# Rotating the query without normalising it, in a local attention of a three-part network

## What is computed

```python
def l2norm(t):
    return t / jnp.clip(jnp.linalg.norm(t, axis=-1, keepdims=True), 1e-12)

qkv = shift_token(x) @ wqkv                     # 8 heads of 64
q, k, v = to_heads(split(qkv))
q = l2norm(q) * qs
k = l2norm(k) * ksc
q, k = rotary_xpos(q, k)        # t * cos * scale + rotate_half(t) * sin * scale
# windows of 64, each looks at itself and the window before it
sim = einsum('bhwid,bhwjd->bhwij', q * 8, k)    # masked by a band
attn = softmax(sim)
out = einsum('bhwij,bhwjd->bhwid', attn, v)
```

## Time and profile before

| | |
|---|---|
| median of 3 runs | 1942.15 us (1931.54 to 1948.5) |
| profiled execution, its own time | 1935.09 us |
| its span | 1933.0 us |
| TensorE, VectorE, ScalarE, GpSimd busy | 81%, 65%, 51%, 58% |
| mean granted TensorE clock | 0.915 of full speed |

### The profile page before, as it was taken

How to read it: one execution, slowest core, us unless ns; L and a number is a source line. 1 busy time by engine, 2 the same in 40 slices (tenths; PEclk the granted TensorE clock), 3 DMA queues, 4 the chain that set the end, 5 groups by cost and what they waited for, 6 DMA issues and landing times.

```text
span 1933.0 us, 31789 instructions
## 1 busy us (share of the span) xinstructions
PE 1569.3 (81%) x12145; PEld 1057.8 (55%) x12153; DVE 1251.9 (65%) x2158; ACT 977.6 (51%) x2359; POOL 1116.3 (58%) x1069
## 2 busy tenths in 40 slices
PE   5688787878788968787989787889797689899866
PEld 3354454546555645465656454656564367677535
DVE  6665564678777855797768557877685454354345
ACT  3266557525555654255465642554656354444333
POOL 0000000777777747777777467777774777777700
PEclk8999899989999989899989988999998799899866
DMA  4010001434333344333334343334343633333311
GB/s 162 5 24 17 14 21 39 111 100 118 115 109 110 116 90 104 97 114 118 107 99 119 77 116 101 105 116 120 101 118 76 181 109 98 103 100 102 102 17 44
DMA packets 93420, 178.72 MB, mean 92 GB/s; under 512 B 21452, under 2 KB 50264, under 8 KB 93016
## 3 DMA queue, kind: packets, MB, share of 16 engines
q0 software_dynamic: 50688, 138.48, 25.3%
q1 hardware_dynamic: 42584, 38.23, 7.1%
HBM read 151.46 MB, written 9.44 MB: 83 GB/s over the span
## 4 chain that ended last, share of the span: by engine, by line
PE 48%; DVE 14%; POOL 13%; ACT 12%; issue 8%; DMA 3%; SPq 1%; DVEq 0%; POOLq 0%; ACTq 0%
POOL pool_c L746 13%; PE c L1630 7%; PE pa L1526 4%; PE pb L1526 3%; PE ta L1560 3%; PE sc L1605 3%; ACT pool_a L788 2%; DMA pool_c<-rows_of_x,idx 2%; PE ta L1534 2%; DVE pool_c L1253 2%; PE tb L1407 2%; PE pa L1578 2%; ACT pool_a L853 1%; PE pa L1568 1%; PE pb L1578 1%
## 5 line engine op out<-in xcount | busy, mean ns | idle before, releaser
L746 POOL DMA_INDIRECT pool_c<-rows_of_x,idx x1056 | 1113.5, 1054 | 723.1 <-DVE pool_c L1341 330.2
L1253 DVE TENSOR_TENSOR pool_c<-pool_c 128x768 f32<-128x768 f32 x352 | 331.8, 950 | 89.8 <-DMA pool_c<-rows_of_x,idx 89.5
L1630 PE MATMUL c<-ident,pool_c 128*128 128x128 f32 x2112 | 307.4, 285 | 56.0 <-DVE pool_c L1253 56.0
L1630 PEld LDWEIGHTS c<-ident,pool_c 128*128 128x128 f32 x2112 | 252.4, 147 | 136.0 <-DVE pool_c L1253 71.6
L877 ACT ACTIVATE prob<-sc,nmax 128x128 f32<-128x128 f32 x512 | 178.8, 373 | 0.2
L788 ACT COPY pool_a<-tb 128x512 f32<-128x512 f32 x188 | 113.7, 605 | 13.7 <-PE tb L1407 7.0
L1526 PE MATMUL pa<-wqkv,pool_a 128*128 128x512 f32 x194 | 107.2, 635 | 14.0 <-DVE pool_a L1203 8.9
L1526 PE MATMUL pb<-wqkv,pool_a 128*128 128x512 f32 x190 | 104.0, 630 | 9.4 <-DVE pool_a L1203 4.6
L877 ACT ACTIVATION_READ_ACCUMULATOR prob<-sc,nmax 128x1 f32 x512 | 109.6, 214 | 0.0
L1150 DVE TENSOR_REDUCE ssq<-pool_a 128x16 f32<-128x1024 f32 x64 | 77.9, 1216 | 38.1 <-ACT pool_a L853 37.6
L853 ACT ACTIVATE pool_a<-pa 128x512 f32<-128x512 f32 x64 | 38.2, 597 | 111.8 <-PE pa L1526 111.7
(11 more groups left out here) (413 smaller groups left out, 3197.2 us busy)
## 6 DMA issues: line engine op xcount, KB each, us to landing
pool_c<-rows_of_x,idx POOLq DMA_INDIRECT x1056
vmix<-vring SPq DMA_DIRECT2D x128, 128.0 KB
rows_of_x<-x2tok SPq DMA_DIRECT2D x16, 256.0 KB
xtok<-in_x SPq DMA_DIRECT2D x4, 512.0 KB, 6.3
x_of_all<-x2tok SPq DMA_DIRECT2D x8, 256.0 KB, 2.9
out<-pool_c SPq DMA_DIRECT2D x8, 256.0 KB, 2.3
wqkv<-in_wqkv SPq DMA_DIRECT2D x1, 1536.0 KB
xtok<-x_of_all SPq DMA_DIRECT2D x3, 512.0 KB, 4.5
```

The costliest lines, as they stand in the source:

```text
L746: pool.indirect_dma_start(gat[:, n % GB, s, :], None, tables[b % 2], bass.IndirectOffsetOnAxis(ap=idx[:, t, SC * c + s:SC * c + s + 1], ax ...
L1253: V.tensor_tensor(g4, g4, wv, ALU.mult).then_inc(SEM["c_prod"], 1)
L1630: ins = mm(out[:, c:c + P], x, ident[:], start=(i == 0 and k == 0), stop=(i == BCH - 1 and k == len(parts) - 1), is_transpose=True, skip_g ...
```

## The change

The query is no longer normalised. At the end of step "proj", in `rotate_query`, VectorE multiplies it out of its bank by sine (into `r2q`, two buffers laid into `xtok`) and by cosine (into `qn`), which frees the bank. Step "rn" multiplies the key alone and copies the query's eight inverse norms to `qinv` (four buffers). Step "rot" rotates the key alone, at half the width. In "S", the negated maxima are multiplied by the inverse norms, with a wait for the reduction. In "X", each exponential has the inverse norm as its scale, beside the bias. SyncE's loads into `xtok` wait for the last turned keys of the batch before, where they waited for `a_y`. Buffer `r2` shrinks to half, and the tiles laid out behind it in `pool_a` move by 512 columns.

```diff
--- before.py
+++ after.py
@@ -426,10 +426,11 @@
...
         uT = xtok.rearrange("p t d -> p (t d)")
+        r2q = uT.rearrange("p (a h d) -> p a h d", a=2, h=HB)
         qn = part("b", 2, 2, INNER)
-        r2 = part("b", 2, HB, DH)
+        r2 = part("b", HB, DH)
         hT = part("b", N)
...
@@ -443,6 +444,7 @@
...
         nmax = sb("nmax", [P, 2, 2, PAIRS])
+        qinv = sb("qinv", [P, 4, HB])
         rsum = sb("rsum", [P, 2, HB])
...
@@ -515,7 +517,7 @@
...
             "b_shift": 8, "b_square": 32, "b_ss": 32, "b_rn": 32, "b_sin": 16, "b_qk": 16,
-            "b_max": 16, "b_recip": 16, "b_mix0": 256, "b_mix1": 256, "b_newton": 48, "c_newton": 8, "f_shift": 9, "f_edge": 1, "f_hn": 4, "f_res": 2,
+            "b_max": 32, "b_qinv": 16, "b_recip": 16, "b_mix0": 256, "b_mix1": 256, "b_newton": 48, "c_newton": 8, "f_shift": 9, "f_edge": 1, "f_hn": 4, "f_res": 2,
             "c_silu": 2, "c_act": 4, "c_pos": 2 * POS, "c_w": T, "c_table0": 48, "c_table1": 48, "c_prod": CHUNKS, "c_acc": CHUNKS - J,
...
@@ -643,7 +645,7 @@
...
-                    wait(sp, "a_y", b - 1, 3)
+                    wait_filled(sp, ("kT", LAYERS - 1, T - 1), b - 1)
                     sp.dma_start(xtok[:], A["batch"](A["x"], b)).then_inc(SEM["x_loaded"], 16)
@@ -681,7 +683,7 @@
...
                 else:
-                    wait(sp, "a_y", B - 1, 3)
+                    wait_filled(sp, ("kT", LAYERS - 1, T - 1), B - 1)
                 sp.dma_start(xtok[:], A["batch"](x3_dram, m)).then_inc(MOE["x3"], 16)
@@ -871,11 +873,12 @@
                     sc = wait_filled(act, ("S", l, n), b)
-                    wait(act, "b_max", b, T * l + n + 1)
+                    wait(act, "b_max", b, 2 * (T * l + n) + 2)
                     for e in range(2):
...
                             ins = nc.scalar.activation(prob[:, n % 2, pr, e, :], sc[:, e, P * pr:P * (pr + 1)], ACT.Exp,
-                                                       bias=nmax[:, n % 2, e, pr:pr + 1], accum_out=rsum[:, n % 2, 2 * pr + e:2 * pr + e + 1])
+                                                       bias=nmax[:, n % 2, e, pr:pr + 1],
+                                                       scale=qinv[:, n % 4, 2 * pr + e:2 * pr + e + 1], accum_out=rsum[:, n % 2, 2 * pr + e:2 * pr + e + 1])
                     ins.then_inc(empty(("S", l, n), b), 1)
...
@@ -1150,6 +1153,7 @@
...
                     V.tensor_scalar(ssq[:, t % 2, 0, :], ssq[:, t % 2, 0, :], 1e-24, None, ALU.max).then_inc(SEM["b_ss"], 1)
+                    rotate_query(b, l, t)
                 elif what == "rn":
...
@@ -1159,6 +1163,9 @@
...
                                     negate=True).then_inc(SEM["b_max"], 1)
+                    wait(dve, "b_qinv", b, T * l + n + 1)
+                    wait(dve, "b_max", b, 2 * (T * l + n) + 1)
+                    V.tensor_tensor(nmax[:, n % 2], nmax[:, n % 2], qinv[:, n % 4].rearrange("p (r e) -> p e r", e=2), ALU.mult).then_inc(SEM["b_max"], 1)
                 elif what == "R":
...
@@ -1198,10 +1205,25 @@
...
                 polish(ssq[:, t % 2, 1, :], ssq[:, t % 2, 0, :], newt[:, 0:16], SEM["b_newton"], lambda k: wait(dve, "b_newton", b, 3 * i + k))
-                for w, key in enumerate((("qp", l, t), ("kp", l, t))):
-                    src = wait_filled(dve, key, b)
-                    V.tensor_tensor(qn[:, t % 2, w, :].rearrange("p (h d) -> p h d", h=HB), src[:, :].rearrange("p (h d) -> p h d", h=HB),
-                                    ap3(ssq[:, t % 2, 1, HB * w:HB * (w + 1)], [[1, HB], [0, DH]]), ALU.mult).then_inc(empty(key, b), 1)
+                src = wait_filled(dve, ("kp", l, t), b)
+                V.tensor_tensor(qn[:, t % 2, 1, :].rearrange("p (h d) -> p h d", h=HB), src[:, :].rearrange("p (h d) -> p h d", h=HB),
+                                ap3(ssq[:, t % 2, 1, HB:2 * HB], [[1, HB], [0, DH]]), ALU.mult).then_inc(empty(("kp", l, t), b), 1)
+                V.tensor_copy(qinv[:, t % 4], ssq[:, t % 2, 1, 0:HB]).then_inc(SEM["b_qinv"], 1)
+
+            def turned_half(x):
+
+                return bass.AP(tensor=x.tensor, offset=x.offset + 32, ap=[x.ap[0], [DH, HB], [-32, 2], [1, 32]])
+
+            def rotate_query(b, l, t):
+
+                i = T * l + t
+                src = wait_filled(dve, ("qp", l, t), b)
+                if i > 1:
+                    wait_filled(dve, ("kT", *divmod(i - 2, T)), b)
+                V.tensor_tensor(r2q[:, t % 2].rearrange("p h (s d) -> p h s d", s=2), turned_half(src[:, :]),
+                                ap3(rot[:, l, t, 1, 0, :], [[0, HB], [32, 2], [1, 32]]), ALU.mult)
+                V.tensor_tensor(qn[:, t % 2, 0, :].rearrange("p (h d) -> p h d", h=HB), src[:, :].rearrange("p (h d) -> p h d", h=HB),
+                                ap3(rot[:, l, t, 0, 0, :], [[0, HB], [1, DH]]), ALU.mult).then_inc(empty(("qp", l, t), b), 1)
@@ -1210,12 +1232,12 @@
...
                     wait_filled(dve, ("kT", *divmod(i - 1, T)), b)
-                own = qn[:, t % 2]
-                V.tensor_tensor(r2.rearrange("p w h (s d) -> p w h s d", s=2), bass.AP(tensor=own.tensor, offset=own.offset + 32, ap=[own.ap[0], [INNER, 2], [DH, HB], [-32, 2], [1, 32]]),
-                                ap3(rot[:, l, t, 1, 0, :], [[DH, 2], [0, HB], [32, 2], [1, 32]]), ALU.mult).then_inc(SEM["b_sin"], 1)
+                own = qn[:, t % 2, 1, :]
+                V.tensor_tensor(r2.rearrange("p h (s d) -> p h s d", s=2), turned_half(own),
+                                ap3(rot[:, l, t, 1, 1, :], [[0, HB], [32, 2], [1, 32]]), ALU.mult).then_inc(SEM["b_sin"], 1)
                 wait(dve, "b_sin", b, i + 1)
-                V.tensor_tensor(own.rearrange("p w (h d) -> p w h d", h=HB), own.rearrange("p w (h d) -> p w h d", h=HB),
-                                ap3(rot[:, l, t, 0, 0, :], [[DH, 2], [0, HB], [1, DH]]), ALU.mult).then_inc(SEM["b_qk"], 1)
+                V.tensor_tensor(own.rearrange("p (h d) -> p h d", h=HB), own.rearrange("p (h d) -> p h d", h=HB),
+                                ap3(rot[:, l, t, 0, 1, :], [[0, HB], [1, DH]]), ALU.mult).then_inc(SEM["b_qk"], 1)
@@ -1529,7 +1551,7 @@
...
                         out = wait_free(pe, (name, l, n), b)
-                        parts = [x[:, P * i:P * (i + 1)] for x in (qn[:, n % 2, w, :], r2[:, w].rearrange("p h d -> p (h d)")) for i in range(PAIRS)]
+                        parts = [x[:, P * i:P * (i + 1)] for x in (qn[:, n % 2, w, :], (r2 if w else r2q[:, n % 2]).rearrange("p h d -> p (h d)")) for i in range(PAIRS)]
                         for k, x in enumerate(parts):
...
```

## The result

| | before | after |
|---|---|---|
| median of 5 runs each | 1942.15 us (1931.54 to 1948.5) | 1960.09 us (1957.05 to 1963.85) |
| profiled execution: span | 1933.0 us | 1958.0 us |
| VectorE busy | 1251.9 us | 1233.2 us |
| ScalarE busy | 977.6 us | 1025.4 us |
| mean granted TensorE clock | 0.915 | 0.911 |

The ratio is 1.0095 with an interval of 1.0068 to 1.0122: 18 us slower, where +28 was forecast. The interval leaves out 1, so the loss is real, but it stays just under the 1% (1961.6 us) that the prediction set as the limit of "no change". New are L1223 and L1225 (the query's products), L1211 (the copy of its inverse norms) and L1168 (the product with the maxima).

A forecast was written before the change was run, and what follows sets the result against it. No engine is full; a ring of hand-overs between engines bounds the kernel. Terms of +4.7, +5.8, +6.9, +12.2, +4.7, -7.4 and +0.6 gave +27.5 us on the median 1942.15: 1970 us, range 1942 to 1990, forecast's own 1959 to 1980.

The forecast's parts named there:

- rival B: Exponentials on ScalarE: the scale column hides behind the accumulator's read-out, so it costs nothing; +17, 1959 us; chance 0.12.
- The price of the scale: ScalarE's eight exponentials per tile: +0.09 us each for the scale column, +0.72 per tile, 46 us of busy time.
- Terms 1 and 2: Longer exponentials on the chain: eight batch 0 tiles at 0.59, +4.7 us; eight crossings where layers meet at 0.72, +5.8.
- The named link: Eight tiles of batch 0: TensorE waits some 0.6 us more at the scores (L1598) for the key copy.
- Term 5: Nine layer 1 tiles, batches 1 to 3, keys' turn behind L1173: six lose 0.33, three lose 0.9; +4.7 us.
- Terms 3 and 4: Query products delay VectorE: five gather crossings, +6.9 us; seventeen layer 0 crossings (batches 1 to 3, joints), +12.2.
- Term 6: Gains: four rotation crossings (-4.9), two first tiles via the query's bank (-1.75), two key-only normalisations (-0.8); together -7.4 us.
- VectorE's busy time: VectorE over 64 tiles: 3.62 us per tile becomes 3.52, 6 us less busy time, within 10 us of before.
- Rival A: Only the exponentials count; GpSimd's rate and VectorE's idle time take up the query products; +4, 1946 us; chance 0.20.
- Rival C: Faster: query's bank comes free early and VectorE's idle time hides the products; 21 us less, 1921 us; chance 0.11.
- Rival D: TensorE's granted clock falls more often; its dearer bound gives the high end, 1990 us; chance 0.15.
- From 1500 us on the same work, only later: Second block and experts at the end: untouched, so the first blocks' loss arrives there almost one for one.

The follow-up runs named there:

- The split of the exponentials: Three of a tile's eight exponentials moved on ScalarE behind the turned query and key copies: 1.0143 on the kernel after, 1.0014 on the kernel before.

## Why the prediction was right, and where its steps were not

The direction and the range held: slower, 1960 within 1942 to 1990 and within the forecast's own 1959 to 1980. That it landed within 10 us of 1970 is in part luck, by two errors of opposite sign: the scale came 4 to 6 us dearer, the rest 13 cheaper. It is luck too that rival B's number, 1959, is the nearest: its mechanism was wrong. By the prediction's own limit of 1961.6 us the result falls on the side "within 1%", which had 0.27.

- **The price of the scale: right.** 0.46 us was forecast for L879, 0.458 measured; ScalarE is 47.8 us busier, 46 forecast. The scale column made an exponential 85 ns longer (373 to 458 ns), with the accumulator's read-out behind each (214 ns before, 205 after). Rival B fell with it.
- **Terms 1 and 2, what the scale costs on the path: too small.** 10.5 us forecast. Measured: 14.5 to 16 within the change, 27 alone. In batch 0 the step is +0.71, not 0.59, and it comes in nine tiles, not eight. I had subtracted 0.13 of the 0.15 us between the key copy and the scores as slack. The gap is still there in the kernel after (the key copy ends at 129.81, the scores start at 129.94), so it was a hand-over and no slack. The tighter link was the copy of the turned query ahead of it, with some 0.05 us to spare; and the scores also need the tile that the exponentials empty. And I had charged only batch 0 and eight joints. With the scale alone 6 us more lie in the layers 1 of batches 1 to 3, at two tiles each, and 14.5 in the three stretches of their layer 0. The size of the latter is uncertain: one slow execution, and chance moves such a stretch by up to 5.2 us.
- **The named link: wrong in its place.** "TensorE waiting some 0.6 us more at L1598 for the key copy" is not what the trace shows: there it rose from 1.2 to 2.7 us in the whole kernel. The wait sits one product earlier, at the turn of the attention output, for the copy of the turned query out of `tb` (L1429, 15.1 us in all, where L1407 had 5.1). The split of the exponentials shows another link behind it.
- **Term 5, nine tiles of layer 1: right in its mechanism.** +0.33 forecast for six, +0.31 to +0.35 measured; but the three with 0.9 took 0.35 as well. 3.1 instead of 4.7. The scale alone doesn't have these steps, the change without the scale has them all, and the late placement removes those of the first two tiles of each layer: that shows the place of the query's products as their cause.
- **Terms 3 and 4, the place in layer 0: right as a price, but set against the wrong credit.** 19.1 forecast, 20.3 measured in the kernel that has the place without the savings, by one profile. Layer 1 loses 9.7 more there, so the place alone was dearer than terms 3 to 5 together. The kernel after, though, loses 13.8 and 7.2 in its two profiles in the layers 0, with the scale's part in it, and 4.5 without the scale. Of the two waits that were to grow, TensorE's for L1253 did (56.0 and 55.5 us before, 62.0 and 59.6 after); its wait for L1173 ahead of the turned keys didn't (8.9 and 6.2 before, 6.2 and 7.2 after).
- **Term 6, the gains: the step that failed.** I gave -7.4 for single crossings, four of them of the rotation. The halved rotation makes every tile's VectorE work behind the norm 1.07 shorter, one normalisation less another 0.6, and the query's bank comes free earlier. The whole change without the scale nets +4 us, while the place alone costs 33: together these savings are worth some 29 us. At which crossings each of them pays, no run isolates. I had written that the saving is small and the order is what counts; I then priced the order of the added work at 22 crossings and the order of the removed work at four.
- **VectorE's busy time**: -6 forecast, -18.7 measured, outside the 10 us that I had allowed. I had taken a count from start to start for busy time. The count itself left out 0.10 us: the second L1203 takes 0.71 until L1214 starts (124.85 to 125.56), so a tile took 3.72 us before, not 3.62. The 0.16 us for a product that waits for the maxima was an estimate that no row shows; in the kernel after L1168 starts 0.11 us behind the end of L1164 (122.02, 122.13). And the whole of the 18.7 is overlap, 88 us before and 107 after: by the sum of durations, 1340 us in both kernels, nothing was saved.
- **Rival A** (only the exponentials count, 1946): without the scale little is left, as it said, but not for its reason. VectorE's idle time did not take up the query's products, since alone they cost 33 us; the savings behind them paid for them. **Rival C** had its one half: the earlier bank takes the wait of 13.5 to 5.7 us, but VectorE's idle time, 25.7 down to 3.9, was spent, not spare. **Rival D** (the granted clock falls more often, and the high end of 1990 rests on it): no run shows how many falls a longer wait brings, nor what one of them costs at the end of the kernel. What the trace of the kernel before has is one stretch behind a wait of 2.03 us, 945.40 to 948.60, with a granted clock of 0.50, in which two products of L1526 take 1.92 us (start 946.86) and the next two 1.08 (start 948.57). In the kernel after the mean granted clock is 0.911 against 0.915 and TensorE is busy 10 us longer in the first profile, 4 in the repeat. Over all executions the granted clock averages 0.912 and 0.913 in the kernel after, 0.916 beside its repeat in the kernel before. The change without the scale has 0.912 too and loses only 4 us, so the clock doesn't simply follow the loss; how much of the loss is clock is open.
- **From 1500 us on the same work, only later**: the shift is 26.6 at tile 63 and 25.0 at the end, in the repeat 19.2 and 17.4. Right.

What stays open: why tiles 20 and 36 start 2.3 us earlier against the ones before them. The delay that the first part has collected by then is given back there, in all variants with the query's products early or late (-1.6 to -2.9), but not with the scale alone at tile 20 (+0.6). At 37 and 51 the repeat of the kernel before does it as well (-2.1 and -2.6), at 20 and 36 it doesn't. One gather takes GpSimd 1.05 us in the kernel before and 1.03 in the kernel after (L746, L748). That the gathers got ahead while the first part was late is only my guess; no run isolates it.

## What to carry to other kernels

When work is moved ahead and work behind it is removed, walk the removed work along the chain with the same care as the added one; here the one repaid nearly all that the other had cost. An operand that made each of 512 instructions 85 ns longer was paid almost in full where its engine closes a ring (0.71 of 0.75 us a tile), and a small gap between two links is no slack until the hand-over itself and every other link have been taken off. A fall of an engine's busy time need not be less work: add up the durations too. Before an instruction with a table of its own is moved between two of another table, count the loads: here there were 12 more, of 1.28 us each.

## What was not expected of the hardware

- Profiles of one kernel agree within 0.02 us per tile in steady stretches and differ by 0.9 to 2.6 us at single places (opening, gathers, some joints), in the two of the kernel after by up to 3.5 us (tile 48); a change of 0.3 us per tile can be read from one trace, though medians of several runs can't tell it.
- A product of 128x512 out of PSUM took 680, 685 and 691 ns (L1225, L1223, L1209), out of SBUF 685 and 692 (L1236, L1239).
- Moving eight exponentials by one place in ScalarE's list cost 5.8% of the kernel, the dearest of all edits, though ScalarE is busy for only half of the span (51% in the kernel before and with this edit).
